# Eight batches of causal attention beside a gated FFN: row scaling of the attention by DMA transfers, the output bias on GpSimd, the maxima sent from ScalarE's queue

## What is computed

```python
xn = layernorm(x)
q, k, v = xn @ wq + bq, xn @ wk + bk, xn @ wv + bv      # 16 heads of 16
q, k = rope(q), rope(k)
attn = softmax(q k^T / 4 + causal mask)                  # per head, 512 x 512
s = (attn @ v, heads side by side) @ wo + bo
g = silu(ffn(xn))                                        # ffn: 256 -> 768, silu(gate) * up, -> 256
out = x + s * g
```

## Time and profile before

| | |
|---|---|
| median of 3 runs | 560.32 us (559.06 to 561.85) |
| the profiled execution's own time | 563.19 us |
| its span, first to last instruction | 561.5 us |
| busy: PE, DVE, ACT, POOL | 493.6, 431.0, 327.9, 284.5 us |
| granted TensorE clock, mean over the span | 0.958 of full speed |
| DMA moved | 68.68 MB, 122 GB/s |

### The profile page before, as it was taken

How to read it: one execution, slowest core, us unless ns; L and a number is a source line. 1 busy time by engine, 2 the same in 40 slices (tenths; PEclk the granted TensorE clock), 3 DMA queues, 4 the chain that set the end, 5 groups by cost and what they waited for, 6 DMA issues and landing times.

```text
span 561.5 us, 14792 instructions
## 1 busy us (share of the span) xinstructions
PE 493.6 (88%) x5733; PEld 388.5 (69%) x5733; DVE 431.0 (77%) x725; ACT 327.9 (58%) x682; POOL 284.5 (51%) x407
## 2 busy tenths in 40 slices
PE   0678699989989999989998999989899999999972
PEld 0456597756768777767777777777778787758632
DVE  4399669858898599947998699867886878977623
ACT  2763346647565848537664757646575558654660
POOL 2114269536654966366737548487347535422430
PEclk9998989999999999989999999999899989979889
DMA  9265310775317645272476322568414435632111
GB/s 302 90 199 142 96 58 4 203 172 136 98 36 227 170 116 170 90 139 66 107 218 179 87 85 59 161 160 243 118 30 88 123 125 170 155 94 59 40 39 37
DMA packets 45895, 68.68 MB, mean 122 GB/s; under 512 B 4976, under 2 KB 20848, under 8 KB 45824
## 3 DMA queue, kind: packets, MB, share of 16 engines
q1 hardware_dynamic: 44736, 66.64, 43.8%
q10 hardware_dynamic: 1088, 1.05, 0.6%
HBM read 38.01 MB, written 29.36 MB: 120 GB/s over the span
## 4 chain that ended last, share of the span: by engine, by line
PE 53%; DVE 20%; DMA 8%; issue 6%; SPq 5%; ACT 4%; POOL 3%; DVEq 0%; ACTq 0%; POOLq 0%
PE ps_w L566 28%; PE ps_w L697 10%; DVE row_max L917 9%; PE ps_w L595 6%; PE ps_w L611 6%; ACT probs L808 2%; DMA q_st<-minus_max 2%; PE ps_w L598 2%; PE ps_w L585 2%; DVE hid L951 2%; DMA hid<-mask_rows 1%; DMA k_st<-parts_k 1%; DVE h_lo L416 1%; SPq L526 1%; DVE hid L956 1%
## 5 line engine op out<-in xcount | busy, mean ns | idle before, releaser
L917 DVE TENSOR_REDUCE row_max<-ps_w 128x2 f32<-128x1024 f32 (+3 forms) x256 | 199.9, 819 | 52.8 <-PE ps_w L598 51.7
L808 ACT ACTIVATE probs<-ps_w 128x512 f32<-128x512 f32 (+1 forms) x384 | 180.8, 537 | 92.7 <-PE ps_w L611 81.7
L1000 POOL TENSOR_SCALAR_AFFINE_SELECT probs<-probs 128x256 f32<-128x256 f32 x256 | 106.9, 436 | 166.9 <-ACT probs L808 166.4
L611 PE MATMUL ps_w<-q_st,k_st 49*128 49x512 f32 (+3 forms) x512 | 80.3, 351 | 14.5 <-DVE row_max L917 5.8
L595 PE MATMUL ps_w<-k_st,q_st 48*128 48x512 f32 (+3 forms) x512 | 81.3, 352 | 11.0 <-DVE hid L951 2.6
L566 PE MATMUL ps_w<-xt_hi,wgu_hi 64*128 64x512 f32 x384 | 85.9, 423 | 1.8 <-DVE wgu_lo L896 1.0
L697 PE MATMUL ps_w<-probs,vals 128*32 128x512 f32 (+3 forms) x1024 | 83.8, 471 | 1.4 <-ACT probs L808 1.1
L566 PE MATMUL ps_w<-xt_lo,wgu_hi 64*128 64x512 f32 x384 | 81.7, 400 | 0.0
L595 PEld LDWEIGHTS ps_w<-k_st,q_st 48*128 48x128 f32 x512 | 52.0, 197 | 29.6 <-issue 9.5
L611 PEld LDWEIGHTS ps_w<-q_st,k_st 49*128 49x128 f32 x512 | 49.1, 190 | 31.0 <-issue 8.4
L697 PEld LDWEIGHTS ps_w<-probs,vals 128*32 128x32 f32 x1024 | 30.8, 116 | 42.6 <-issue 33.8
(11 more groups left out here) (100 smaller groups left out, 903.6 us busy)
## 6 DMA issues: line engine op xcount, KB each, us to landing
parts_q<-high_low SPq DMA_DIRECT2D x48, 256.0 KB, 3.7
q_st<-parts_q SPq DMA_DIRECT2D x64, 192.0 KB, 3.7
k_st<-parts_k SPq DMA_DIRECT2D x64, 192.0 KB, 4.5
parts_k<-high_low SPq DMA_DIRECT2D x42, 256.0 KB, 4.1
xn<-L_attn_x SPq DMA_DIRECT2D x8, 512.0 KB, 5.2
res<-L_attn_x SPq DMA_DIRECT2D x8, 512.0 KB, 5.1
result<-res SPq DMA_DIRECT2D x8, 512.0 KB, 3.3
parts_k<-h_hi SPq DMA_DIRECT2D x6, 256.0 KB, 3.4
```

Of the source, the lines that this page charges most:

```text
L611: last = pe.matmul(dst[j][:, col:col + SEQ - t * P], k_st[rows, pair, t * P:(t + 1) * P], q_st[rows, pair, t * P:SEQ], start=True, stop=True)
L808: nc.scalar.activation(probs[:, (pair % 2) * SLOTS + slot, col:col + WIDTH[c]], w_of(kind, b, 3 * pair + c // 2, c % 2)[:, 0:WIDTH[c]], AC ...
L917: last = nc.vector.tensor_reduce(of_pair, both_of(kind, b, i)[:, :, col:col + (t + 1) * P], AX.X, ALU.max)
L1000: nc.gpsimd.affine_select(out=v, in_=v, compare_op=ALU.is_ge, fill=0.0, base=0, pattern=[[0, 2], [1, P]], channel_multiplier=-1).then_inc( ...
```

## The change

For batches 0 to 6 (`BY_PE` = 7) `ON` and the two turnings of `AT` go. The unscaled `o_t` is already transposed, so SP sends its four blocks of 16 rows straight into `attn` (`NA`), and its four rows of sums to DRAM; `NB` reads the sums back as 128 x 16, DVE takes reciprocals (`RC`), `NC` writes them to DRAM, `ND` reads each row back 16 times over into `at_lo`, and DVE multiplies (`AM`). ScalarE then splits from SBUF. Each waits for the landing of the one before. `NA` waits for the copy of `o_t`; ScalarE's next copy into `o_t` waits for all five transfers of `NA`; `ND` waits for both `OP` of the batch before. Batch 7 keeps the way through PE.

The bias: ScalarE scales bo once (`BO`); for each half of a batch GpSimd multiplies gate by bo into `rope_t` and adds it to `res` (`GB`, two instructions) before the `OP` of DVE, which is one instruction now and waits for `bias_added`; so does `AD`.

`MD` is issued by ScalarE, at a written place after `MT`, mostly four or five exponentials later. All five orders are written anew; `RP` items of GpSimd do two steps in one, with the same instructions.

```diff
+BY_PE = BATCH - 1
 ORDER = {
     "sp": """
 ...
-        RD2.2 WS1.3 MD1.2 RD3.2 WS2.3 WS3.3 MD2.2 ST0.1 XL0.5 RD0.3 RD1.3 RL0.2 MD3.2 WS0.4 MD0.3 WS1.4 RD2.3 MD1.3 RD3.3 WS2.4 WS3.4 RD0.4
 ...
+        NB2.2 NA3.2 NB3.2 NC2.2 RL0.2 NC3.2 ND2.2 ND3.2 RD3.3 NA0.3 WS2.4 WS3.4 NB0.3 ST0.2 NC0.3 XL0.6 RD0.4 NA1.3 NB1.3 RD1.4 NC1.3 RD2.4
+        ND0.3 NA2.3 ND1.3 WS0.5 NB2.3 NA3.3 NB3.3 NC2.3 RL0.3 NC3.3 ND2.3 ND3.3 RD3.4 WS1.5 WS2.5 NA0.4 NB0.4 WS3.5 ST0.3 XL0.7 NA1.4 NC0.4
 ...
     "act": """
 ...
+        B33.1 HI1.3 B34.1 QK2.3 B35.1 B36.1 QK3.3 B37.1 PV2.1 B38.1 B39.1 B40.1 B41.1 B42.1 B43.1 MT0.2 G0.3 B44.1 B45.1 B46.1 B47.1 MD0.2
 ...
@@ -308,6 +312,7 @@
 ...
         inv_sum = sb("inv_sum", [P, 2, 2 * TT], F32)
+        sums = sb("sums", [P, 2, 16], F32)
@@ -335,6 +340,9 @@
 ...
                     for which in "qk"] for n in range(2)]
+        sum_rows = nc.dram_tensor("sum_rows", (GROUPS, 4, SEQ), F32, kind="Internal").ap()
+        inv_rows = nc.dram_tensor("inv_rows", (GROUPS, 4, SEQ), F32, kind="Internal").ap()
@@ -388,6 +398,10 @@
 ...
+        def attn_of(k):
+            return attn[:, 2 * k:2 * k + 2, :].rearrange("p t d -> p (t d)"), at_lo[:, k, :].bitcast(F32)
@@ -417,8 +431,7 @@
 ...
             need(eng, prod_ready, 2 * b + i + 1)
-            if i == 0:
-                need(eng, res_in, 16 * (b + 1))
+            need(eng, bias_added, 2 * b + i + 1)
@@ -525,11 +538,37 @@
 ...
                                          by_row[a, :, 2 * i:2 * i + 2, :]).then_inc(stacked[i], 16)
-                elif kind == "MD":
-                    need(sp, max_ready, GROUPS * b + i + 1)
-                    for a in range(2):
-                        row = q_st[64 * a + STACK:64 * a + STACK + 1, 2 * i:2 * i + 2, :].bitcast(F32).rearrange("o n (t c) -> o (n t) c", c=P)
-                        sp.dma_start(row, minus_max[32 * a:32 * a + 2 * TT, i % 2, :].bitcast(F32)).then_inc(max_placed[i % 2], 16)
+                elif kind == "NA":
+                    g, k = b * GROUPS + i, i // 2
+                    need(sp, o_t_ready, g + 1)
+                    need(sp, inv_stored[i % 2], 16 * (g // 2 - 1))
+                    sp.dma_start(sum_rows[i], o_t[HD:P:32, :]).then_inc(sums_stored, 16)
+                    need(sp, at_ready, KT * (b - 1) + k + 1)
+                    if b == 0 and i == 0:
+                        sp.wait_ge(start_rope_done, 9)
+                        sp.wait_ge(raw_ready, 4)
+                        sp.wait_ge(rope_done, 3)
+                    raw = attn_of(k)[0]
+                    for hh in range(4):
+                        at = 64 * (i % 2) + HD * hh
+                        sp.dma_start(raw[at:at + HD, :], o_t[32 * hh:32 * hh + HD, :]).then_inc(raw_placed, 16)
+                elif kind == "NB":
+                    g = b * GROUPS + i
+                    need(sp, sums_stored, 16 * (g + 1))
+                    need(sp, inv_ready, g - 1)
+                    sp.dma_start(sums[:, i % 2, :], sum_rows[i].rearrange("h (p j) -> (h p) j", j=16)).then_inc(sums_in[i % 2], 16)
+                elif kind == "NC":
+                    g = b * GROUPS + i
+                    need(sp, inv_ready, g + 1)
+                    need(sp, inv_placed[i // 2], 32 * b)
+                    sp.dma_start(inv_rows[i].rearrange("h (p j) -> (h p) j", j=16), sums[:, i % 2, :]).then_inc(inv_stored[i % 2], 16)
+                elif kind == "ND":
+                    g, k = b * GROUPS + i, i // 2
+                    need(sp, inv_stored[i % 2], 16 * (g // 2 + 1))
+                    need(sp, prod_ready, 2 * b)
+                    at = 64 * (i % 2)
+                    rows = inv_rows[i].rearrange("h (a c) -> h a c", a=1).broadcast_to([4, HD, SEQ])
+                    sp.dma_start(attn_of(k)[1][at:at + 64, :], rows).then_inc(inv_placed[k], 16)
@@ -764,6 +803,9 @@
                 elif kind == "SL":
 ...
                     nc.scalar.copy(causal[:], hid[:, 0, 0:3 * P]).then_inc(mask_ready, 1)
+                elif kind == "BO":
+                    act.wait_ge(bias_in, 16 * 4)
+                    nc.scalar.activation(bo_row[:], bo_row[:], ACT.Identity, scale=0.5 * WSCALE).then_inc(bo_scaled, 1)
@@ -799,6 +841,12 @@
 ...
                                          scale=-1.0).then_inc(max_ready, 1)
+                elif kind == "MD":
+                    need(act, max_ready, GROUPS * b + i + 1)
+                    for a in range(2):
+                        row = q_st[64 * a + STACK:64 * a + STACK + 1, 2 * i:2 * i + 2, :].bitcast(F32).rearrange("o n (t c) -> o (n t) c", c=P)
+                        act.dma_start(row, minus_max[32 * a:32 * a + 2 * TT, i % 2, :].bitcast(F32)).then_inc(max_placed[i % 2], 16)
@@ -809,9 +857,19 @@
 ...
                 elif kind == "PV":
-                    need(act, pv_done, (b * GROUPS + i + 1) * TT)
+                    g = b * GROUPS + i
+                    need(act, pv_done, (g + 1) * TT)
+                    if g <= GROUPS * BY_PE:
+                        need(act, sums_stored, 16 * g)
+                        need(act, raw_placed, 64 * g)
 ...
                 elif kind == "AT":
+                    if b < BY_PE:
+                        need(act, scaled, KT * b + i + 1)
+                        if b:
+                            need(act, prod_ready, 2 * b)
+                        nc.scalar.copy(at_hi[:, i, :], attn_of(i)[0]).then_inc(at_hi_ready, 1)
+                        return
@@ -916,11 +974,20 @@
 ...
                     last.then_inc(a_taken, 1)
+                elif kind == "RC":
+                    need(dve, sums_in[i % 2], 16 * ((b * GROUPS + i) // 2 + 1))
+                    nc.vector.reciprocal(sums[:, i % 2, :], sums[:, i % 2, :]).then_inc(inv_ready, 1)
+                elif kind == "AM":
+                    need(dve, inv_placed[i], 32 * (b + 1))
+                    need(dve, raw_placed, 64 * (b * GROUPS + 2 * i + 2))
+                    raw, inv = attn_of(i)
+                    nc.vector.tensor_tensor(raw, raw, inv, ALU.mult).then_inc(scaled, 1)
                 elif kind == "ON":
 ...
                     g = b * GROUPS + i
-                    need(dve, attn_ready, g)
+                    need(dve, attn_ready, i)
+                    need(dve, at_ready, KT * b)
@@ -931,17 +998,15 @@
 ...
                 elif kind == "AT":
                     need(dve, at_hi_ready, b * KT + i + 1)
+                    if b < BY_PE:
+                        nc.vector.tensor_tensor(at_lo[:, i, :], attn_of(i)[0], at_hi[:, i, :].bitcast(F32), ALU.subtract).then_inc(at_ready, 1)
+                        return
 ...
                 elif kind == "OP":
 ...
                     ps = w_of(kind, b, 0, i)
-                    by_tile = lambda ap: ap.rearrange("p (a d) -> p a d", d=DM)
-                    if b == 0 and i == 0:
-                        dve.wait_ge(bias_in, 16 * 4)
-                    nc.vector.tensor_tensor(by_tile(ps[:, :]), by_tile(ps[:, :]), by_tile(bo_row[:]).broadcast_to([P, 2, DM]), ALU.add)\
-                        .then_inc(sum_ready, 1)
-                    need(dve, sum_ready, 2 * b + i + 1)
+                    need(dve, bias_added, 2 * b + i + 1)
@@ -987,7 +1054,27 @@
                 elif kind == "RP":
 ...
                         pool.wait_ge(const_in, 16)
+                    if i % 3 == 1 and rope_t_used:
+                        need(pool, *rope_t_used[-1])
                     rotate(pool, nc.gpsimd.tensor_tensor, b, i, rope_t[:])
+                    if i % 3 == 1:
+                        rotate(pool, nc.gpsimd.tensor_tensor, b, i + 1, rope_t[:])
+                        rope_t_used.append(rope_at(b, i // 6, i % 6 + 2))
+                elif kind == "GB":
+                    if b == 0 and i == 0:
+                        pool.wait_ge(bo_scaled, 1)
+                    need(pool, silu_ready, 2 * b + i + 1)
+                    need(pool, *rope_t_used[-1])
+                    need(pool, bias_added, 2 * b + i)
+                    by_tile = lambda ap: ap.rearrange("p (a d) -> p a d", d=DM)
+                    nc.gpsimd.tensor_tensor(by_tile(rope_t[:]), by_tile(gate[:, b % 2, i, :]), by_tile(bo_row[:]).broadcast_to([P, 2, DM]), ALU.mult)\
+                        .then_inc(gate_biased, 1)
+                    need(pool, gate_biased, 2 * b + i + 1)
+                    if i == 0:
+                        need(pool, res_in, 16 * (b + 1))
+                    r = res[:, 2 * i:2 * i + 2, :].rearrange("p t d -> p (t d)")
+                    nc.gpsimd.tensor_tensor(r, r, rope_t[:], ALU.add).then_inc(bias_added, 1)
+                    rope_t_used.append((bias_added, 2 * b + i + 1))
```

(21 more changed lines are left out.)

225 lines of the change are left out of this document (111 added, 114 removed).

## The result

The changed kernel is **slower**, by little: 572.3 us in the median against 561.1 for the kernel before, ratio 1.0135 (95% interval 1.0075 to 1.0194, clear of 1). The ratio sets aside executions in the slower of two states into which a kernel's executions fall, so it is smaller than the quotient of the medians, 1.020. The forecast was 548 us, 2.2% faster; the value lies outside the range of 533 to 567.

What follows compares the result with a forecast made beforehand. PE was taken as the bound, DVE a close second; PE -17.9, DVE -2, bias +2.4 and -1.4, maxima +4.4 and -3, SP +5 gave -12.5 from 563.2, 550.7, times 0.995: 548 us, range 533 to 567.

Steps and rivals of the forecast that it cites:

- So it is hidden, with 2 us to spare there: Way from o_t to OP: some 18 us with queueing, against 20.2 us available in batch 6, the tightest.
- -12.5: Sum of all terms in us: -17.9 - 2 + 2.4 - 1.4 + 4.4 - 3 + 5.
- PE's transposes: Removed ON and AT on PE: 19.1 us of busy time, -17.9 us of path, bounds about -9 to -23.
- my first part: Opening on what bounds the kernel: a hole in PE is paid for again behind it through a lower clock.
- DVE: DVE's work: 31.8 us removed, some added, net -11.9 us busy; taken as -2 us, bounds 0 to -3.1.
- the rule: DVE instructions with two SBUF inputs exclude GpSimd's SBUF reads: 9 us instead of 3, sum 1 to 2 us higher.
- The bias on GpSimd: Bias moved to GpSimd: +2.4 us for masks held up (0 to 5.4), -1.4 us at the end.
- The maxima: Maxima on ScalarE's queue: +4.4 us for issues (0 to 8.4), -3 us for shorter PE weight-load waits (0 to -6.4).
- SP's new work: SP's queue: eight transfers for each of 28 groups, 120 us of issuing; taken as +5 us, bounds 0 to 13.
- SP comes late: Rival: RD3 or WS behind ND3 in SP's queue, stacks late, 4.1 us each time; +25, 573 us, chance 0.18.
- DVE takes over: Rival: PE's 19 us come back as waits for row maxima on DVE; 558 us, chance 0.15.

Runs made afterwards that it cites:

- a_unused: Changed kernel running the whole way of the sums, but DVE neither reads nor waits for the inverse rows (division left out, batches 0 to 6); 0.9759 of before.
- a_wait: a_unused with one line put back: DVE waits for the inverse rows' transfer before each product, still without reading them; 1.0038 of the kernel before.
- a_nosum: Changed kernel without the sums' store, reload, reciprocal and broadcast; blocks of o_t still moved, division left out in batches 0 to 6; 0.9736 of the kernel before.
- a_issues: a_nosum plus four transfers a group from SP, constant data to DRAM, with no wait before or behind them; 0.9684 of the kernel before.
- a_late0: Changed kernel with only the first pair's product and copies and the second group's reciprocal placed later; 1.0177 of the kernel before.
- b3_tr: Kernel before, in its own order, with only the attention scaled through transfers in place of transposes in batches 0 to 6; 1.1546 of the kernel before.
- b1_md: Kernel before, in its own order, with only the maxima sent from ScalarE's queue, directly behind the copy that makes them; 1.0291 of the kernel before.
- ghost_sp: Kernel before with all its work, plus the same eight SP transfers a group, constant data to DRAM that no engine waits for; 1.0152 of before.

## Why the prediction was wrong

- **The step that failed** is the one on the way from `o_t` to `OP`: "So it is hidden, with 2 us to spare there". Its length was near (18 us estimated; 14 to 23 to the product, 17 to 27 to the low part), and against `OP`, its last reader, it was hidden: PE's waits for the low part are 4.8 us, 3.8 before. But the way passes through DVE twice, for the reciprocal and for the product, and then through ScalarE, at fixed places of orders that also carry the row maxima and the exponentials. I wrote that otherwise "PE, DVE and ScalarE wait in their orders" and gave that no price. `a_unused` and `a_wait` price one of these waits at 2.8%, some 16 us; the whole way of the sums costs 4% (`a_nosum`), 22 us. How those 16 us arise inside the orders stays open. -12.5 and 22 give +9.5; measured were +7.6. That they meet so closely is in part luck: the 22 us hold again reciprocals and issues that are in the -12.5, and several terms of that sum were wrong in size or sign, as follows.
- **PE's transposes** were a few us too large, and two fifths of what went was given back through the clock. Busy time times mean clock gives about one amount of work for one list of instructions: with the 5397 instructions of the changed kernel, 471.1 us at a clock of 0.969, 484.4 at 0.946 and 490.9 at 0.932 (`a_issues`, the changed kernel, `a_late0`) make 456.5, 458.2 and 457.5, and 14 of the 15 kernels with that list lie between 456.4 and 459.8 (`b3_tr` has 462.8). The five with the 5733 of before lie between 470.2 and 472.9. So 13 to 15 us of work at full clock went, 14 to 15 at the clock of before, where I took 19.1 of busy time and 17.9 of the path. The fall of the clock from 0.958 to 0.946 takes 6 of it back, and 9.2 us of busy time are left. That holes are paid twice stood in my first part, and the term did not carry it.
- **DVE**: busy time fell by 7.2 us, not 11.9. h_lo went from 807 to 881 ns and `AM` takes 930 where I took 807. The traces tie the rise to the bias on GpSimd: h_lo takes 755 to 820 ns in the seven kernels that add the bias on DVE (GpSimd busy for 284 to 291 us) and 833 to 899 in the thirteen that add it on GpSimd (325 to 339 us); in the changed kernel's own order, with only the bias put back (`bias_dve`), it is 806 against 881. Row maxima, which read PSUM, take 815 to 820 in all twenty. The direction is that of the rule of the Trainium skill's "SBUF — State Buffer" (Who interferes with whom). Its size lies between my two figures: in the changed kernel `AM` (930) and the subtraction into `at_lo` (862) stand 0.24 and 0.17 us over the 0.69 of the form with one operand in PSUM, 5.7 us for the 28, where the row gave 3 and the rule 9.
- **The bias on GpSimd**: the two instructions take 1.39 and 1.37 us, near the 1.28. The weight loads' wait for masks grew by 4.8 us, twice the +2.4 and under the bound of 5.4 (PE's own rows add 3.0); alone it cost 0.75%, 4.2 us, against my +1.0. Beside the transfers it gained 1.9% (`bias_dve`), in an order written for it.
- **The maxima**: the waits for q_st<-minus_max were to vanish and grew from 6.4 to 10.3 us; -3 was wrong in sign. Alone in the old order the part cost 2.9%, 16 us, where my worst case was 8.4. Beside the transfers the same part gained 2%. I had argued both ends with averages of the chain. The sign changes between the two orders; whether the place or what else stands in the two queues does that, no run says. The places do differ, and not as I wrote ahead: in the changed order 20 of the 32 pairs stand at most one exponential behind `MT`, the others two to eight, while `b1_md` has 26 with none between and six with one. What an issue does to ScalarE the trace does show:

```profile
130.90 0.66 ACTq L848 DMA_DIRECT2D q_st<-minus_max  x1
131.09 0.88 ACT L856 ACTIVATE probs<-ps_w 128x512 f32<-128x512 f32 x2
...
207.40 1.28 ACTq L848 DMA_DIRECT2D q_st<-minus_max  x2
208.79 0.66 ACT L856 ACTIVATE probs<-ps_w 128x256 f32<-128x256 f32 x2 [0.93 <-issue]
```

  Exponentials handed over earlier still start during an issue (131.09), and what stands behind it in the list begins after it (208.79). Of the 43 us of idle time that I expected there, 6.4 are put to issue.
- **SP's new work**: +5 (0 to 13) stands: 8.5 us in `ghost_sp`, nothing measurable in `a_issues`. The rival "SP comes late" forecast the sign, not the cause: the waits for k_st grew by 3 us on the weight loads (5.7 to 8.7) and by 5 in PE's own row (2.5 to 7.7), but `a_unused`, at 0.976, still has 6.9 and 5.7 of them, and SP's standing costs at most 1.5%.
- **The range** reached to 567 on that rival alone. (Its neighbour, "DVE takes over", comes to 556 and not 558: half way is 558.7 before the factor of 0.995.) A wait added to DVE's order, the second engine of the chain, had no rival of its own.

## What to carry to other kernels

A chain of dependent transfers is judged not by its last reader, but by every engine that takes a step of it in a fixed order, and by what stands behind that step. A wait of 11 us in total there cost 16 us of the end; another, of 13, cost 8 at most, so such a wait is to be measured and not scaled. PE's holes are to be counted with the clock they cost: busy time times granted clock shows the work that was really removed. And a part put alone into an order made for other work measures the place it was given as well; take one wait or one operand away instead.
